# First loads in another order, a warm-up on TensorE, and the bias rows last, in a four-layer graph network kernel

## The chip, the cores and the metric

The kernel runs on one core of one Trainium2 chip. The metric is the device time of one execution in microseconds. The kernel before takes 1088.81 us (median of 3 runs, 1088.4 to 1089.32).

## The reference, cut to what matters

The reference puts 256 nodes with 768 features through four graph layers, each followed by `x = layernorm(x + layer(x))`. Only the very beginning of the first layer matters here, and four of its inputs:

```python
# 4352 edges: src, dst (0..255), edge_type_3 (0..2), edge_type_34 (0..33)
c = segment_sum(m.astype(x.dtype), dst)              # per relation: edges that end in a node
...
qg = einsum('blf,gf->blg', q, Wg[:, F:]) + bg        # q: query_embs, 8 x 64 rows of 768
hg = einsum('bnf,gf->bng', h3, Wg[:, :F])
attn = sigmoid(hg[:, :, None, :] + qg[:, None, :, :])
```

The kernel starts with two things that need nothing else: the query product `qg` (512 rows by 768, times 768 by 768, plus the bias `bg`) and the matrix of edge counts (destination by source, 256 x 256, for each of three relations).

## The kernel before, in words

Every engine has its own program, written out by hand, and semaphores tie them together. No planner sets the order: what stands earlier in an engine's list is done earlier. SyncE (SP) issues nearly all loads; all of them go through one hardware queue.

**SP.** It first issues four loads of 17 KB into `keys` (`src`, `dst`, `t3`, `t34`; L331), then `qT[0]` (the first 256 query rows, turned; 768 KB; L354; this buffer shares its memory with `MT[0]`, the name in the profile), then the first weight `W[0]` in three column thirds of 768 KB (L363), then `qT[1]` (L354) and the next weight `W[1]` (2304 KB, L365). After that it waits for buffers to come free.

**VectorE (DVE).** It waits for the four key loads, turns them into float32 (L1512 to L1516), and builds two one-hot tables of 34 chunks: `S1` by source (L1518) and `E[1]` by destination, relations 0 and 1 packed into one number (L1519). Each pair of chunks raises `chunk_ready`. Then it builds `E[0]` for relation 2 (34 instructions, L1507), and then it unpacks the sums that TensorE left in banks 6 and 7: for each bank it runs L1529 (from PSUM), L1530 (from SBUF to SBUF), L1531 (with one input from PSUM), and raises `half_read`. Two additions (L1533, L1534) finish the counts. After these come the low halves of the query rows (L1548, `query_lo`), the normalised counts (L1539 to L1541), a low half of x (L1562), another table of one-hots (L1507), tables for the last layer (L1567 to L1577), `query_lo` again, and the low halves L1555.

**TensorE (PE).** It waits for `bg_ready`, adds the bias into banks 0 to 5 by eight small products (L618), multiplies `qT[0]` by `W[0]` third by third (`natural3`, L581, 36 products that the trace shows as 72 records), raises `q_done`, adds up the counts of the chunks into banks 6 and 7 (L629, 68 matmuls), waits for `half_read`, and does the same for relation 2 in bank 6 (L637, 68 matmuls). Then come the sums of the counts (L643), the second half of the query product (L581) with one more sum in its middle (L569, which waits until the first two relations are normalised), and the first product of the layer (L668).

**ScalarE (ACT).** It rounds the bias (L1198), then waits for `q_done` and for `W[1]`, and splits off the high parts of the first two thirds of `W[1]` (L1193), then of x (L1205), and copies the query rows (L1207).

**GpSimd (POOL).** It makes constants: `iotab` (L395, raises `consts` to 1), masks and the identity (L397 to L417). It takes the low part of the bias (L421, raises `bg_ready`), waits for the last third of `W[0]` (`w_in[0]`), loads x (L424, L425), and then computes the low parts of the thirds of `W[1]`, as soon as ACT has made the high ones (`third_lo_first`, L430, whole inputs and output in SBUF, 128 x 1536).

`keep_busy(count, bank)` issues that many matmuls of 128 x 256 on the index table `iotab`; nobody reads what they leave.

Of the kernel before, what the change touches and what calls it, by code (L numbers as in the profile page):

```python
# [38 lines left out]
NODES, FEAT, EDGES = 256, 768, 4352  # L39
NT = NODES // P  # L40
KC = FEAT // P
EC = EDGES // P
# [36 lines left out]
def by_pool(n):  # L79

    return (n + 1) // 4
R3, R34 = 3, 34
HEADS1 = 4
SLOPE, MASKED = 0.2, 1e30
# [2 lines left out]
THIRD = FEAT // 3  # L87
# [10 lines left out]
def build(nc, A):  # L98
    with ExitStack() as ctx:
# [3 lines left out]
        def sem(name):  # L103
            return ctx.enter_context(nc.semaphore(name))


        PS = ctx.enter_context(nc.psum_tensor("PS", [P, 8, 512], F32))
        at_w = (nc.sbuf_base + 63) // 64 * 64
        W = [sb(f"W{i}", [P, KC, FEAT]) for i in range(2)]
# [4 lines left out]
        hN, hT = sb("hN", [P, NT, FEAT]), sb("hT", [P, KC, NODES])  # L114
# [5 lines left out]
        BG = nc.alloc_sbuf_tensor_at("BG", [33, FEAT], F32R, offset=at_h + 1024 * 20)  # L120
# [18 lines left out]
        keys = sb("keys", [P, 4, EC], I32)  # L139
# [110 lines left out]


        keys_in, x_in, bg_in, small_in, out_done = (sem(n) for n in ("keys_in", "x_in", "bg_in", "small_in", "out_done"))
        q_in = [sem("q_in0"), sem("q_in1")]
        first_in = [sem("first_in0"), sem("first_in1")]
        w_in = [sem("w_in0"), sem("w_in1")]
        rel_w_in = [[sem(f"rel_w_in{j}{q}") for q in range(2)] for j in range(2)]
        qd_in = [sem("qd_in0"), sem("qd_in1")]
# [69 lines left out]
        @block.sync  # L327
        def _(sp):

            for i, n in enumerate(("src", "dst", "t3", "t34")):  # L330
                sp.dma_start(keys[:, i, :], A[n].rearrange("(p c) -> p c", c=EC)).then_inc(keys_in, 16)  # L331
            def queries(g, u, h):

                for j in range(4):
                    sp.dma_start(QD[h][HQ * j:HQ * j + HQ, :], A["qU"][u, HQ * h:HQ * h + HQ]).then_inc(qd_in[h], 16)

            for m, w in enumerate(stream):
                if m in (6, 13):
                    g = m // 13
                    if g == 0:  # L340
                        sp.wait_ge(slot_found, EC)
                    else:
                        sp.wait_ge(wl_used, 3 * (R3 + 1))
                    for h in range(2):
                        queries(g, 0, h)
                if m in (9, 16):
                    g = m // 16
                    for u, h in product(range(1, UNITS), range(2)):
                        past = g * STEPS + (u - 1) * UB + (h + 1) * QUADS
                        sp.wait_ge(prod_done, by_dve(past))  # L350
                        sp.wait_ge(pool_prod, by_pool(past))
                        queries(g, u, h)
                if m < 2:
                    sp.dma_start(qT[m][:], turned(A["qT"])[:, :, m * NODES:(m + 1) * NODES]).then_inc(q_in[m], 16)  # L354
                elif m in (3, 4, 5, 6):
                    sp.wait_ge(wr_used, 3 * (m - 2))
                    sp.sem_inc(w_used, 1)
                else:
                    sp.wait_ge(w_used, m - 1)
                if m == 0:  # L360
                    for q in range(3):
                        cols = slice(q * THIRD, (q + 1) * THIRD)
                        sp.dma_start(W[0][:, :, cols], turned(w)[:, :, cols]).then_inc(w_in[0] if q == 2 else first_in[q], 16)  # L363
                else:
                    sp.dma_start(W[m % 2][:], turned(w)).then_inc(w_in[m % 2], 16)  # L365
            for n in range(2 * R34):
                r, q = divmod(n, 2)
                if n < 4:
                    if q == 0:
                        sp.wait_ge(w_used, FIRST34 - 1 + r)  # L370
                else:
                    sp.wait_ge(w_lo, n - 3)
                cols = slice(q * HALF, (q + 1) * HALF)
                sp.dma_start(W[(FIRST34 + r) % 2][:, :, cols], turned(A["L3_rel"][r])[:, :, cols]).then_inc(rel_w_in[r % 2][q], 16)
            m = FIRST34 + R34
            sp.wait_ge(w_lo, 2 * R34 - 2)
            sp.dma_start(W[m % 2][:], turned(A["L3_gcn"])).then_inc(w_in[m % 2], 16)

            for t in range(NT):
                sp.wait_ge(ln_done, 2 * 3 + t + 1)  # L380
                sp.dma_start(A["out"][t * P:(t + 1) * P, :], xN[:, t, :]).then_inc(out_done, 16)
            sp.wait_ge(out_done, 16 * NT)
# [110 lines left out]
        def _(pe):  # L493
# [3 lines left out]
            def keep_busy(count, bank):  # L497

                for _ in range(count):
                    pe.matmul(PS[:, bank, 0:NODES], iotab[:, 0:P], iotab[:], start=True, stop=True)  # L500
# [68 lines left out]
                    mm = pe.matmul(PS[:, bank, 0:NODES], ones[:], cnt[:, s, :], start=s == 0, stop=s == NT - 1)  # L569
                mm.then_inc(deg_spread, 1)  # L570

            def natural3(T, Wm, bank=0, first=False, last=False, tiles=range(NT), thirds=range(3), ready=None):

                for t in tiles:
                    for q in thirds:
                        at = 3 * t + q
                        out = PS[:, bank + at // 2, (at % 2) * THIRD:(at % 2 + 1) * THIRD]
                        for k in range(KC):
                            if ready and at == 0 and k % 2 == 0:
                                ready(k // 2)  # L580
                            mm = pe.matmul(out, T[:, k, t * P:(t + 1) * P], Wm[:, k, q * THIRD:(q + 1) * THIRD],  # L581
                                           start=first and k == 0 and at % 2 == 0,
                                           stop=last and k == KC - 1 and at % 2 == 1, skip_group_check=True)
                return mm

            def aggregate(n, x, nrm):
# [25 lines left out]
                return mm  # L612


            pe.wait_ge(bg_ready, 1)
            for u in range(2):
                for bank, at, f, n in ((0, 0, 0, 512), (1, 0, 512, 256), (1, 256, 0, 256), (2, 0, 256, 512)):
                    pe.matmul(PS[:, 3 * u + bank, at:at + n], ROWS2[:], BG[:, f:f + n], start=at == 0, stop=False,  # L618
                              skip_group_check=True)
            pe.wait_ge(q_in[0], 16)  # L620
            for q in range(3):
                pe.wait_ge(w_in[0] if q == 2 else first_in[q], 16)
                mm = natural3(qT[0], W[0], last=True, thirds=[q])
            mm.then_inc(q_done, 1)
            for c in range(EC):
                h, i = divmod(c, EHALF)
                pe.wait_ge(chunk_ready, c + 1)
# [14 lines left out]
            for s in range(NT):  # L642
                mm = pe.matmul(PS[:, 7, :], ones[:], CNT[:, 0:2, s, :], start=s == 0, stop=s == NT - 1)  # L643
            mm.then_inc(deg_spread, 2)
            pe.wait_ge(q_in[1], 16)
            natural3(qT[1], W[0], bank=3, last=True, tiles=[0])
            spread_counts(2, CNT[:, 2], bank=7)
            natural3(qT[1], W[0], bank=3, last=True, tiles=[1]).then_inc(w_used, 1)
            pe.wait_ge(qg_ready, 4)
# [50 lines left out]
            for g in range(2):  # L700
# [49 lines left out]
                weights(m0 + 4)  # L750
                if g == 0:
                    pe.wait_ge(slot_found, EC)
                natural3(hT, W[(m0 + 4) % 2], bank=3, first=True, last=True,
                         ready=lambda j: pe.wait_ge(relu_done, 3 * g + j + 1)).then_inc(w_used, 1)
                if g == 0:
                    sort_edges()
# [1333 lines left out]
```

## Time and profile before

| | |
|---|---|
| median of 3 runs | 1088.81 us |
| profiled execution | 1089.91 us |
| its span, first to last instruction | 1088.2 us |
| PE busy | 1039.5 us (96%) |
| DVE busy | 764.1 us (70%) |
| ACT busy | 573.4 us (53%) |
| POOL busy | 263.4 us (24%) |
| mean granted TensorE clock | 0.994 |

All rows come from one profiled execution. Times are counted from the first instruction. "Busy" counts an engine from the start to the modelled end of its instructions, so a busy PE may still be slow. The change is at the start, so the views of the first 85 us are the ones to read: which engine the chain of waits runs over, and what each engine waited for.

### The profile page before, as it was taken

To read this page: it belongs to the slowest core of one execution; us is meant where nothing else is said; L and a number is where in the kernel's file an instruction comes from. 1 tells how busy PE (TensorE), PEld (TensorE's weight loads), DVE (VectorE), ACT (ScalarE), POOL (GpSimd) and SP (SyncE) were. 2 spreads that over 40 slices of the span, in tenths; PEclk is the share of its full clock that TensorE was granted. 3 is DMA by queue.
4 is the path that set the end of the run, shared out by engine and by line. 5 is a ranking of instruction groups with operands and counts; after the bars stand their busy time and mean duration, and the time that the engine had idled before them with its cause. 6 is when DMAs were issued, how large, how long until landed. Compare 5 with 4: busy or idle time off the path is not lost.

```text
span 1088.2 us, 17713 instructions
## 1 busy us (share of the span) xinstructions
PE 1039.5 (96%) x7444; PEld 858.3 (79%) x7444; DVE 764.1 (70%) x1092; ACT 573.4 (53%) x606; POOL 263.4 (24%) x160
## 2 busy tenths in 40 slices
PE   6999999999999999999999989989999999999987
PEld 5889986454699984455879689956999999999974
DVE  8793855888654238887644584745989998989862
ACT  0432226888533248887324363324667676766630
POOL 3524705999300038996100000000000000000000
PEclk9999999999999999999999999999999999999999
DMA  8043247212043373220424302604978787877830
GB/s 296 12 135 129 88 149 230 59 59 59 2 174 123 119 220 130 60 59 20 160 88 175 117 1 87 246 11 138 304 256 283 256 284 256 270 261 263 276 118 29
DMA packets 82291, 163.18 MB, mean 150 GB/s; under 512 B 4044, under 2 KB 60136, under 8 KB 81918
## 3 DMA queue, kind: packets, MB, share of 16 engines
q1 hardware_dynamic: 80736, 151.86, 41.4%
q0 software_dynamic: 1472, 10.15, 3.4%
q8 instruction: 60, 0.98, 0.4%
q14 instruction: 23, 0.19, 0.1%
HBM read 158.35 MB, written 0.80 MB: 146 GB/s over the span
## 4 chain that ended last, share of the span: by engine, by line
PE 80%; DVE 13%; issue 4%; ACT 2%; POOL 1%; DVEq 0%; POOLq 0%; ACTq 0%
PE PS L1089 20%; PE PS L770 8%; PE PS L941 7%; PE PS L786 5%; PE PS L692 5%; PE PS L581 4%; PE PS L1072 4%; PE PS L511 4%; PE PS L668 4%; PE PS L524 3%; PE PS L593 3%; PE PS L1105 2%; PE PS L1006 2%; PE PS L828 2%; DVE PRD L1677 1%
## 5 line engine op out<-in xcount | busy, mean ns | idle before, releaser
L1926 DVE TENSOR_TENSOR Wlo<-W,Whi 128x2304 fp32r<-128x2304 f32 x68 | 172.1, 2551 | 19.0 <-ACT Whi L1425 19.0
L1425 ACT CAST Whi<-W 128x2304 fp32r<-128x2304 f32 x68 | 144.5, 2127 | 0.2 <-DMA W<-in_L_rel 0.2
L1089 PE MATMUL PS<-Whi,Mhi 128*128 128x384 f32 x408 | 138.0, 338 | 0.0
L1089 PE MATMUL PS<-Wlo,Mhi 128*128 128x384 f32 x408 | 136.5, 335 | 0.0
L1089 PE MATMUL PS<-Whi,Mlo 128*128 128x384 f32 x408 | 136.5, 334 | 0.0
L478 POOL TENSOR_TENSOR PRDP<-arena 128x1024 f32<-128x1024 f32 x48 | 114.8, 2391 | 30.1 <-issue 17.9
L770 PE MATMUL PS<-QH,SEL 128*128 128x512 f32 x384 | 115.7, 422 | 5.3 <-ACT xT L1262 1.4
L1283 ACT ACTIVATE arena<-PS 128x1024 f32<-128x1024 f32 x96 | 98.4, 1025 | 23.6 <-PE PS L770 23.5
L770 PEld LDWEIGHTS PS<-QH,SEL 128*128 128x128 f32 x384 | 64.8, 188 | 55.2 <-DVE PRD L1677 21.3
L1283 ACT ACTIVATE PS<-PS 128x1024 f32<-128x1024 f32 x96 | 97.9, 1019 | 2.6 <-PE PS L770 2.6
L1089 PEld LDWEIGHTS PS<-Whi,Mhi 128*128 128x128 f32 x408 | 76.8, 188 | 0.4 <-DVE Wlo L1926 0.2
L1089 PEld LDWEIGHTS PS<-Whi,Mlo 128*128 128x128 f32 x408 | 76.9, 188 | 0.0
L1089 PEld LDWEIGHTS PS<-Wlo,Mhi 128*128 128x128 f32 x408 | 76.6, 188 | 0.0
L1677 DVE TENSOR_TENSOR PRD<-PS,arena 128x1024 f32<-128x1024 f32 x48 | 58.5, 1220 | 19.7 <-ACT PS L1283 19.7
L1677 DVE TENSOR_TENSOR arena<-PS,arena 128x1024 f32<-128x1024 f32 x48 | 58.6, 1220 | 11.7 <-ACT PS L1283 11.7
L941 PE MATMUL PS<-WThi,Thi 128*128 128x256 f32 x216 | 61.5, 285 | 0.7 <-DVE Tlo L1804 0.7
L430 POOL TENSOR_TENSOR WR<-W,WH 128x1536 fp32r<-128x1536 f32 x12 | 48.6, 4058 | 52.3 <-ACT WH L1193 52.3
L941 PE MATMUL PS<-WThi,Tlo 128*128 128x256 f32 x216 | 61.1, 283 | 0.0
L941 PE MATMUL PS<-WTlo,Thi 128*128 128x256 f32 x216 | 61.1, 283 | 0.0
L1437 ACT CAST Mhi<-PS 128x512 fp32r<-128x512 f32 x51 | 30.0, 588 | 54.5 <-PE PS L1072 54.5
L1794 DVE TENSOR_TENSOR WTlo<-W,WThi 128x1536 fp32r<-128x1536 f32 x18 | 31.6, 1756 | 33.6 <-ACT WThi L1337 33.6
L1072 PE MATMUL PS<-BB,Xhi 128*128 128x256 f32 x204 | 52.0, 289 | 0.5 <-DVE Mlo L1955 0.5
(296 smaller groups left out, 2430.3 us busy)
## 6 DMA issues: line engine op xcount, KB each, us to landing
W<-in_L_rel SPq DMA_DIRECT2D x68, 1152.0 KB, 6.4
W<-in_W_rel SPq DMA_DIRECT2D x6, 2304.0 KB, 9.3
W<-in_W SPq DMA_DIRECT2D x6, 2304.0 KB, 9.4
arena<-in_qU SPq DMA_DIRECT2D x96, 128.0 KB, 2.6
W<-in_WqT SPq DMA_DIRECT2D x4, 2304.0 KB, 9.7
W<-in_W_root SPq DMA_DIRECT2D x2, 2304.0 KB, 13.5
W<-in_WgT SPq DMA_DIRECT2D x2, 2304.0 KB, 9.7
QH<-QH POOLq DMA_DIRECT2D x2, 1536.0 KB, 9.9
```

The costliest lines, as they stand in the source:

```text
L430: nc.gpsimd.tensor_tensor(part, third_turned(W[(1 + w // 3) % 2], w % 3), WH[(w + 1) % 3][:].bitcast(F32), ALU.subtract).then_inc(wr_ready, 1)
L478: nc.gpsimd.tensor_tensor(PRDP[k % 2], SIGP, QD[h], ALU.mult).then_inc(pool_prod, 1)
L692: mm = pe.matmul(PS[:, q, c * NODES:(c + 1) * NODES], WL[b][w % 2][:, k, c, :], TS[a][:, k, :], start=p == 0 and k == 0 and a == b == 0 an ...
L770: mm = pe.matmul(PS[:, at_banks(c) + b // 2, :], SEL[:, i, :], QH[h][:, u, b:b + 2, :].rearrange("p b f -> p (b f)"), start=True, stop=True)
L786: mm = pe.matmul(PS[32 * b:32 * b + 32, 6 + u % 2, 0:THIRD], RED[:, i % QUADS, :], made[:, b * THIRD:(b + 1) * THIRD], start=i == 0, stop= ...
L941: mm = pe.matmul(PS[:, bank + at // 2, (at % 2) * THIRD:(at % 2 + 1) * THIRD], TS[a][:, k, t * P:(t + 1) * P], WT[b][w % 2][:, k, :], star ...
L1072: mm = pe.matmul(PS[:, 6 + i % 2, kk * NODES:(kk + 1) * NODES], XS[part][:, t, k * P:(k + 1) * P], BB[:, t * NODES:(t + 1) * NODES], start ...
L1089: mm = pe.matmul(PS[:, 4 + s % 2, 0:HALF], MS[a][mb][:, k, j * P:(j + 1) * P], WS[b][w % 3][:, k, :], start=n == 0, stop=n == 17)
L1283: nc.scalar.activation(out, sums, ACT.Sigmoid).then_inc(attn_done, 1)
L1425: nc.scalar.copy(WS[0][w % 3][:], W[(FIRST34 + r) % 2][:, :, q * HALF:(q + 1) * HALF]).then_inc(w_hi, 1)
L1677: V.tensor_tensor(PRD[k % 4], sig, QD[h], ALU.mult).then_inc(prod_done, 1)
L1926: V.tensor_tensor(WS[1][w % 3][:], W[(FIRST34 + r) % 2][:, :, q * HALF:(q + 1) * HALF], WS[0][w % 3][:].bitcast(F32), ALU.subtract).then_i ...
```

## The change

In SP's program the first loads are `qT[0]` and the first third of `W[0]` for the first two of six feature blocks (256 KB each), then the four key loads, then the other four blocks of both, then the second and the last third of `W[0]`. In TensorE's program 16 filler matmuls into bank 7 come first. They wait for `iotab` alone. The query product follows, its first third in two pieces, and the eight bias products stand at its end, where `bg_ready` is now waited for. Bank starts are given by the new argument `opens`. In the code below, `natural3` has no `first` any more.

```diff
+FIRST_KS = (range(2), range(2, KC))
...
-        q_in = [sem("q_in0"), sem("q_in1")]
-        first_in = [sem("first_in0"), sem("first_in1")]
+        q_in, third_in = sem("q_in"), sem("third_in")
+        first_in = [sem(f"first_in{j}") for j in range(2)]
...
-            for i, n in enumerate(("src", "dst", "t3", "t34")):
-                sp.dma_start(keys[:, i, :], A[n].rearrange("(p c) -> p c", c=EC)).then_inc(keys_in, 16)
...
-                if m < 2:
-                    sp.dma_start(qT[m][:], turned(A["qT"])[:, :, m * NODES:(m + 1) * NODES]).then_inc(q_in[m], 16)
+                if m == 1:
+                    sp.dma_start(qT[1][:], turned(A["qT"])[:, :, NODES:2 * NODES]).then_inc(q_in, 16)
+                elif m == 0:
+                    for j, ks in enumerate(FIRST_KS):
+                        ks = slice(ks[0], ks[-1] + 1)
+                        sp.dma_start(qT[0][:, ks, :], turned(A["qT"])[:, ks, 0:NODES]).then_inc(first_in[j], 16)
+                        sp.dma_start(W[0][:, ks, 0:THIRD], turned(w)[:, ks, 0:THIRD]).then_inc(first_in[j], 16)
+                        if j == 0:
+                            for i, n in enumerate(("src", "dst", "t3", "t34")):
+                                sp.dma_start(keys[:, i, :], A[n].rearrange("(p c) -> p c", c=EC)).then_inc(keys_in, 16)
...
                 if m == 0:
-                    for q in range(3):
+                    for q in range(1, 3):
                         cols = slice(q * THIRD, (q + 1) * THIRD)
-                        sp.dma_start(W[0][:, :, cols], turned(w)[:, :, cols]).then_inc(w_in[0] if q == 2 else first_in[q], 16)
+                        sp.dma_start(W[0][:, :, cols], turned(w)[:, :, cols]).then_inc(w_in[0] if q == 2 else third_in, 16)
...
-            pe.wait_ge(bg_ready, 1)
-            for u in range(2):
-                for bank, at, f, n in ((0, 0, 0, 512), (1, 0, 512, 256), (1, 256, 0, 256), (2, 0, 256, 512)):
-                    pe.matmul(PS[:, 3 * u + bank, at:at + n], ROWS2[:], BG[:, f:f + n], start=at == 0, stop=False,
-                              skip_group_check=True)
-            pe.wait_ge(q_in[0], 16)
-            for q in range(3):
-                pe.wait_ge(w_in[0] if q == 2 else first_in[q], 16)
-                mm = natural3(qT[0], W[0], last=True, thirds=[q])
-            mm.then_inc(q_done, 1)
+            pe.wait_ge(consts, 1)
+            keep_busy(16, 7)
+            for j, ks in enumerate(FIRST_KS):
+                pe.wait_ge(first_in[j], 32)
+                natural3(qT[0], W[0], opens=(0, 3), thirds=[0], ks=ks)
+            pe.wait_ge(third_in, 16)
+            natural3(qT[0], W[0], opens=(4,), thirds=[1])
+            pe.wait_ge(w_in[0], 16)
+            natural3(qT[0], W[0], thirds=[2])
             pe.wait_ge(bg_ready, 1)
+            bias_rows(0, False)
+            bias_rows(3, True).then_inc(q_done, 1)
```

## Rows read from the trace of the kernel before

**Rows 1.** The page, part 1: busy time, share of the span, instructions.
```profile
PE 1039.5 (96%) x7444; PEld 858.3 (79%) x7444; DVE 764.1 (70%) x1092; ACT 573.4 (53%) x606; POOL 263.4 (24%) x160
```
**Rows 2.** The chain of waits, 0 to 84 us: start, duration, what.
```profile
9.89 2.92 PE PS L618 x8
12.82 17.70 PE PS L581 x72
30.51 7.44 PE PS L629 x68
...
81.55 1.99 PE PS L593 x8
```
**Rows 3.** Timeline, 5 to 42 us, VectorE: start, duration, line, operation, idle before.
```profile
4.78 0.23 DVE L1512 CAST keyf<-keys 128x136 f32<-128x136 int32 x1 [3.84 <-DMA keys<-in_t]
8.11 1.82 DVE L1518 TENSOR_SCALAR S<-iotab,keyf 128x256 bf16<-128x256 bf16 x1
23.72 6.75 DVE L1507 TENSOR_SCALAR E<-iotab,ekey 128x256 bf16<-128x256 bf16 x34
34.26 0.69 DVE L1529 TENSOR_SCALAR NRM<-PS 128x512 f32<-128x512 f32 x1 [3.79 <-PE PS L629]
34.99 0.85 DVE L1530 TENSOR_SCALAR CNT<-NRM 128x512 f32<-128x512 f32 x1
...
37.97 0.69 DVE L1529 TENSOR_SCALAR NRM<-PS 128x512 f32<-128x512 f32 x1 [1.41 <-PE PS L629]
38.70 0.73 DVE L1530 TENSOR_SCALAR NRM<-NRM 128x512 f32<-128x512 f32 x1
41.62 7.11 DVE L1548 TENSOR_TENSOR QH<-PS,QH 32x1536 fp32r<-32x1536 f32 x4
```
**Rows 4.** DMA, 0 to 60 us: issues, KB each, median us to landing.
```profile
W<-in_WgT SPq DMA_DIRECT2D x3, 768.0 KB, 9.3
W<-in_W_root SPq DMA_DIRECT2D x1, 2304.0 KB, 18.3
```
**Rows 5.** Timeline, the first 12 us, SP: start of issue, duration.
```profile
0.81 0.38 SPq L331 DMA_DIRECT2D keys<-in_src  x1
2.65 0.43 SPq L354 DMA_DIRECT2D MT<-in_qT  x1
```
**Rows 6.** Line 354, both loads of qT: the time to landing.
```profile
DMA to landing us min/median/max: 5.6/8.2/10.7
```
**Rows 7.** Timeline, 30 to 40 us, ScalarE.
```profile
30.55 2.85 ACT L1193 CAST WH<-W 128x1536 fp32r<-128x1536 f32 x2 [25.18 <-PE PS L581]
```
**Rows 8.** Timeline, GpSimd, 5 to 11 and 30 to 40 us.
```profile
7.94 1.90 POOL L421 TENSOR_TENSOR BG<-biasN,BG 1x768 fp32r<-1x768 f32 x1
32.11 7.03 POOL L430 TENSOR_TENSOR WR<-W,WH 128x1536 fp32r<-128x1536 f32 x2 [14.64 <-ACT WH L1193]
```
**Rows 9.** Line 430, whole span: duration ns min/median/max, first and last start.
```profile
L430 POOL TENSOR_TENSOR WR<-W,WH x12: 3437/3486/10267, 32.1 to 128.4; 128x1536 fp32r<-128x1536 f32 x12
```
**Rows 10.** Timeline, 112 to 132 us: VectorE, then GpSimd.
```profile
114.53 4.68 DVE L1617 TENSOR_TENSOR PROW<-iota,t34f 128x4352 bf16<-128x4352 f32 x1
119.13 2.55 DVE L1619 TENSOR_TENSOR PCOL<-iota,t34f 128x2312 bf16<-128x2312 f32 x1
...
114.72 17.16 POOL L430 TENSOR_TENSOR WR<-W,WH 128x1536 fp32r<-128x1536 f32 x3
```
**Rows 11.** Windows: us, busy PE, PEld, DVE, ACT, POOL, granted clock, DMA.
```profile
13.00:14.00 1.00, 1.00 (x3) 0.82 (x4) 1.00 (x6) 0.00 (x0) 0.00 (x0) 1.00 1.10 347
18.00:19.00 1.00, 1.00 (x6) 0.87 (x6) 1.00 (x6) 0.00 (x0) 0.00 (x0) 1.00 1.02 390
...
307.00:308.00 1.00, 1.00 (x6) 1.00 (x6) 1.00 (x1) 0.00 (x0) 0.00 (x0) 0.50 1.01 409
```
**Rows 12.** Timeline, TensorE, around 306 us and around 55 us.
```profile
306.22 0.39 PE L692 MATMUL PS<-Thi,WLhi 128*128 128x256 f32 x1 [1.85 <-DVE Tlo L1705]
...
54.69 1.10 PE L569 MATMUL PS<-CNT,ones 128*128 128x256 f32 x4
```

More of the change, by code:

```diff
@@ L570, in spread_counts, with natural3 @@
                 mm.then_inc(deg_spread, 1)
-            def natural3(T, Wm, bank=0, first=False, last=False, tiles=range(NT), thirds=range(3), ready=None):
+            def natural3(T, Wm, bank=0, opens=(), last=False, tiles=range(NT), thirds=range(3), ks=range(KC), ready=None):
                 for t in tiles:
@@ L577, in natural3 @@
                         out = PS[:, bank + at // 2, (at % 2) * THIRD:(at % 2 + 1) * THIRD]
-                        for k in range(KC):
+                        for k in ks:
                             if ready and at == 0 and k % 2 == 0:
@@ L581, in natural3, with bias_rows @@
                             mm = pe.matmul(out, T[:, k, t * P:(t + 1) * P], Wm[:, k, q * THIRD:(q + 1) * THIRD],
-                                           start=first and k == 0 and at % 2 == 0,
+                                           start=k == 0 and at in opens,
                                            stop=last and k == KC - 1 and at % 2 == 1, skip_group_check=True)
+                return mm
+            def bias_rows(bank, opens):
+                for b, at, f, n in ((0, 0, 0, 512), (1, 0, 512, 256), (1, 256, 0, 256), (2, 0, 256, 512)):
+                    mm = pe.matmul(PS[:, bank + b, at:at + n], ROWS2[:], BG[:, f:f + n], start=opens and at == 0,
+                                   stop=not opens and (b, at) != (1, 0), skip_group_check=True)
                 return mm
@@ L644, in _ @@
             mm.then_inc(deg_spread, 2)
-            pe.wait_ge(q_in[1], 16)
-            natural3(qT[1], W[0], bank=3, last=True, tiles=[0])
+            pe.wait_ge(q_in, 16)
+            natural3(qT[1], W[0], bank=3, tiles=[0])
             spread_counts(2, CNT[:, 2], bank=7)
@@ L752, in _ @@
                     pe.wait_ge(slot_found, EC)
-                natural3(hT, W[(m0 + 4) % 2], bank=3, first=True, last=True,
+                natural3(hT, W[(m0 + 4) % 2], bank=3, opens=(0, 2, 4), last=True,
                          ready=lambda j: pe.wait_ge(relu_done, 3 * g + j + 1)).then_inc(w_used, 1)
```

## The prediction
> **What bounds the kernel now.** I read the page first: TensorE is busy for 96% of the span [rows 1], so it looks like the bound everywhere. The change touches only the first 40 us, and there the chain of waits says more. It runs over TensorE up to 37.95 us (bias products from 9.89, query product from 12.82 to 30.51, count sums 7.44 us) and then passes to VectorE; it comes back to TensorE only at 81.55 us, at L593 [rows 2]. Between these two points the chain is one row after another of VectorE, without a gap. So TensorE's start is worth only what it brings forward on VectorE at 38 us. What is saved there goes through to L593, and after 81.55 us TensorE hardly waits.
>
> The VectorE timeline shows where the slack is: it waits 3.84 us for the keys, and 3.79 us for bank 6 before L1529 [rows 3]. Before the second L1529, for bank 7, it waits 1.41 us more [rows 3]. Together 5.2 us is all that an earlier TensorE can give.
>
> **TensorE's side.** The filler starts once `iotab` stands, near 1.8 us. A warm L629 takes 7.44 / 68 = 0.109 us from one to the next [rows 2]; at half the clock 0.22, so 16 take 3.5 us, to 5.3 us. The rate before shows the cold start: 3 records in a microsecond at 13 us, 6 at 18 us [rows 11], so the product runs at 1.2 GHz until about 17 us although TensorE began at 9.89. Warm, a record takes about 0.216 us from one to the next, so a product (two records) takes 0.43, and the 72 records 15.5 us instead of 17.7 [rows 2].
>
> The data come as follows. `qT[0]`, issued at 2.65, landed 5.6 us later, at 8.25 [rows 5, 6], which is the shortest of the two times. The middle third of `W[0]` took 9.3 us from its issue [rows 4] and landed near 13.0; the thirds came 2.3 us apart (10.7, 13.0, 15.3), the time of 768 KB in a full queue. Now the stream starts with the first big load at 0.81 instead of 2.65 (1.8 us earlier), and the keys are put into it (about 0.6 us): everything after them lands about 1.2 us earlier, the last third near 14.1. The first piece lands near 5.5, and its 4 products are done before the second piece lands near 9.5. From there the work binds: 32 products of 0.43 us, to 23.3, then the bias products, 2.92 us before at the low clock [rows 2], half of that warm: `q_done` near 24.7 instead of 30.5. The chunk sums end near 32.1 instead of 37.95, and bank 6 is ready near 28.4.
>
> **VectorE's side, the keys.** The four key loads were issued from 0.81 on, 0.46 us apart, and had landed for L1512 at 4.78 [rows 3, 5]. Now two issues of that length stand ahead of them (0.9 us) and 512 KB in the same queue. The bounds are 0.9 us later (issue alone) and 3.5 us (landing at 8.25, like `qT[0]` with more bytes ahead). By the rate of the first loads, about 270 GB/s, 512 KB are 1.9 us from about 2.6 us on; with 0.6 for the keys and the time to landing that gives 5.9 instead of 4.7: 1.2 us later. VectorE gets about 0.2 back, because fewer of its first instructions meet GpSimd's masks. I take the tables to end 1.0 us later: L1507's table at T = 31.5 instead of 30.47 [rows 3].
>
> If nothing else happened, VectorE would go on at T without waiting: 2 x 1.95 us for the two banks and 1.3 us for the additions, and L1548 would start at T + 5.3 = 36.8 instead of 41.62: a gain of 4.8 us.
>
> **What is late next: GpSimd's two instructions of L430.** I think that this gain is lost. L430 stands after ACT's L1193, and that waited for `q_done` until 30.55 [rows 7]. `W[1]` had landed at 9.16 + 18.3 = 27.5 [rows 4]. With `q_done` at 24.7 the load decides: it lands near 26.5, ACT's first copy takes 1.47, and L430 is issued near 28 us, in the middle of VectorE's table. In the rows before, these two engines exclude each other for some operations: L1518 took 1.82 us, against 0.28 for its neighbours, beside L421 (7.94 to 9.84) [rows 3, 8]; L1530 took 0.85 and 0.73 us, and each ended 0.29 us after the end of one of the two L430 (about 35.56 and 39.14) [rows 3, 8]. L1530 (SBUF to SBUF) is hit; L1529 and L1531, which read PSUM, are not. The one-hots of L1507 are the same form as L1518.
>
> Who goes first? At 114.72 an L430 was issued beside L1617, and L1619 was started while L1617 ran; GpSimd took 10.27 us in place of 3.49 [rows 9, 10], so it got in only at 121.5, when both were over. VectorE's unbroken run kept it out. L1507 is such a run. So the first L430 gets in at T and holds to T + 3.45. VectorE: L1529 to T + 0.75; L1530 waits and ends at T + 3.75; L1531 to T + 4.45, `half_read`. The second L430 gets in after L1530 and ends near T + 7.2; the second L1530 ends near T + 7.45. From there to L1548 it is 41.62 - (38.70 + 0.73) = 2.2 us as before [rows 3]: T + 9.6 = 41.1 instead of 41.62. **The gain on VectorE is 0.5 us.** ACT's query copies are done by then.
>
> The Trainium skill (SBUF — State Buffer, Who interferes with whom) has this as an exclusive lock on a port pair that VectorE and GpSimd share, held for a whole instruction: copies, casts and tensor_scalar in the two-port modes take it, and "Issue order, not op shape, decides who blocks". The blocked rows agree. By issue order alone L430 would get in at 28 us, between two one-hots; that is the second rival, and the row at 114.72 speaks against it.
>
> **TensorE again.** It is idle from 32.1 to T + 4.5 = 36.0, 3.9 us. At 306.22 it had waited 1.85 us and the clock then stood at 0.50 for about 3.4 us [rows 11, 12], which costs 1.7. The sums L637 then end at 36.0 + 7.4 + 1.7 = 45.1, as before (they began near 37.7, when L629 ended). L569 started at 54.69 [rows 12], when VectorE had just normalised relation 1; TensorE gets there no earlier than before, so VectorE's third L1539 loses 0.1 us of its gain. Without the drop of the clock all 0.5 us stay; with twice the price 1.3 us are lost instead. I take 0.4 us.
>
> The sum: the profiled execution of 1089.91 (span 1088.2) becomes 1089.5; it lay 1.1 us above the median. The median 1088.81 becomes **1088.4 us**. About 0.2% (2.2 us) is what a measurement of this kernel can tell from no change.
>
> **Rivals.**
> *No blocking worth the name.* The two L430 slip past both L1530. For it: the blocking is inferred from five rows, and between two instructions of VectorE there may be room that no row here shows. Against it: the two L430 are 6.9 us of GpSimd, and from their issue at 28 us to the last addition of VectorE there are only 9 us. VectorE gains 4.8 us; TensorE gains less, 33.8 instead of 37.7 at L637, and if its clock drops in the 1.7 us gap, 2.2 us. VectorE's third L1539 waits for L569 and follows: a gain of 2.5 to 4.2 us, 1084.6 to 1086.3, say 1085.3.
>
> *GpSimd gets in first* (the other side). The first L430 takes the pair at 28 us and stalls the table for 3.45 us: T becomes 34.9. The second waits for the end of the run and hits L1530: `half_read` at T + 4.5 = 39.4 instead of 36.6, L637 starts 1.75 us later than before, cold after 7 us of idling (1.7 more). L569 and the third L1539 are then 3.1 us late, and that reaches L593 over VectorE [rows 2]: 1088.8 + 3.1 = 1091.9. It decides as soon as one L430 starts inside the L1507 run. If both do, 1093.
>
> *The first piece lands late.* Then the filler only fills and the product starts near 9.5 as before; TensorE has 3.9 us to spare before `half_read`, so the time is that of the forecast. It is inside it.
>
> **How the numbers follow.** The forecast 0.55 (own range 1086.7 to 1090.3: keys 0.9 to 3.5 us later shift T by as much, and the clock costs 0 to 3.4 us), no blocking 0.30, GpSimd first 0.15. The range of 8 in 10 reaches half into both: 1084.8 to 1091.0. Faster by over 0.2%: 0.30. Within: 0.55. Slower: 0.15.
>
> **What would show it.** L1512 near 6.0 us. The end of the query product (ACT's L1193 no longer waits for it) near 24.7. L430 issued near 28 us with a duration near 7 us instead of 3.45 (if GpSimd gets in first: a duration of 3.45, and one L1507 of 3.5 us). The first L1530 near 3 us long. L637 at 36. L1548 near 41.1. Wrong if L1548 starts before 39 or after 43, or if the shift at 41.6 us is not the one at L593.

## The result, and the profile after

The changed kernel takes 1093.38 us (median of 6 runs, 1091.58 to 1094.83), the kernel before 1088.90 beside it (6 runs, 1088.02 to 1089.35): ratio 1.0041, 95% interval [1.0030, 1.0052]. It is 4.5 us **slower**. The forecast was 1088.4, no change; the result lies above its range (1084.8 to 1091.0) and on the figure of the second rival with both low parts inside the table (1093). The change is small, 0.4%, but the interval keeps clear of 1.

The profiled execution is the fastest of the six (1091.58, span 1089.8). Read it for the first 90 us. The delay found there lasts nearly to the end: SyncE issues its last weight load at 1045.71 us, 3.9 us after the kernel before (1041.81). In the last 45 us this execution won 2.2 us back. The change touches nothing there, and executions of one kernel differ by 1.3 to 6 us here; why these two differ at that place is open.

The page's part 1, after. Beside [rows 1] VectorE is busy for 6.1 us more, with the same 1092 instructions: some of them take longer.
```profile
PE 1041.8 (96%) x7460; PEld 858.2 (79%) x7460; DVE 770.2 (71%) x1092; ACT 573.4 (53%) x606; POOL 262.9 (24%) x160
```
The chain of waits, 25 to 90 us, after (start, duration, what).
```profile
25.60 13.27 DVE E L1523 x34
...
40.86 9.40 PE PS L653 x68
50.26 1.73 PE PS L659 x4
...
54.27 2.11 DVE NRM L1557
...
86.22 1.99 PE PS L607 x8
```
This part of the chain starts on VectorE (before it stands the keys' load, up to 7.11 us, and VectorE's work on the keys), with the table of 34 one-hots (L1507 before, L1523 here) at almost twice its 6.75 us. At the end stands the product that began at 81.55 [rows 2]; here it begins at 86.22, **4.67 us later**, about what the medians differ by.

VectorE's timeline, 3 to 56 us, after (start, duration, line, operation, idle before). The lines answer to L1512, L1516, L1507, L1529 to L1531, L1548 and L1541 before.
```profile
7.21 0.23 DVE L1528 CAST keyf<-keys 128x136 f32<-128x136 int32 x1 [6.28 <-DMA keys<-in_t]
8.04 1.66 DVE L1532 TENSOR_SCALAR ekey<-keyf 128x34 f32<-128x34 f32 x1
...
38.79 0.68 DVE L1545 TENSOR_SCALAR NRM<-PS 128x512 f32<-128x512 f32 x1
39.51 0.43 DVE L1546 TENSOR_SCALAR CNT<-NRM 128x512 f32<-128x512 f32 x1
...
41.53 0.43 DVE L1546 TENSOR_SCALAR NRM<-NRM 128x512 f32<-128x512 f32 x1
...
44.15 7.11 DVE L1564 TENSOR_TENSOR QH<-PS,QH 32x1536 fp32r<-32x1536 f32 x4
...
54.27 2.11 DVE L1557 TENSOR_TENSOR NRM<-CNT,RC 128x512 f32<-128x512 f32 x1
```
Both waits for TensorE are gone (3.79 and 1.41 us in [rows 3]), and both SBUF copies L1546 take 0.43 us, not 0.85 and 0.73. The step that the prediction was built on did not happen there. It happened earlier. First line L1523's own view, then the timeline of VectorE and GpSimd in two slices of a few tenths of a us:
```profile
L1523 DVE TENSOR_SCALAR E<-iotab,ekey x34: 273/274/3548, 25.6 to 38.6; 128x256 bf16<-128x256 bf16 x34
```
```profile
28.94 3.55 DVE L1523 TENSOR_SCALAR E<-iotab,ekey 128x256 bf16<-128x256 bf16 x1
28.96 3.44 POOL L437 TENSOR_TENSOR WR<-W,WH 128x1536 fp32r<-128x1536 f32 x1 [11.69 <-ACT WH L1209]
...
32.37 3.48 POOL L437 TENSOR_TENSOR WR<-W,WH 128x1536 fp32r<-128x1536 f32 x1
32.41 3.52 DVE L1523 TENSOR_SCALAR E<-iotab,ekey 128x256 bf16<-128x256 bf16 x1
```
The shortest, median and longest one-hot: 273, 274 and 3548 ns. Two of 34 took 3.5 us, and each ends within 0.1 us of the end of a low part. GpSimd got in at once, with 3.44 and 3.48 us. Between the two low parts VectorE got exactly one one-hot through.

TensorE, the first 51 us, after.
```profile
1.77 3.60 PE L507 MATMUL PS<-iotab 128*128 128x256 bf16 x16 [1.77 <-POOL iotab L402]
5.16 2.84 PE L588 MATMUL PS<-W,MT 128*128 128x256 f32 x8
10.00 15.77 PE L588 MATMUL PS<-W,MT 128*128 128x256 f32 x64 [2.00 <-DMA W<-in_WgT]
25.70 1.67 PE L596 MATMUL PS<-BG,ROWS 33*128 33x512 f32 x8
...
40.86 9.40 PE L653 MATMUL PS<-E,S 128*128 128x256 bf16 x68 [5.96 <-DVEq L1548]
```
The product and the bias rows end at 27.4, not at 30.5. TensorE then idles 5.96 us for the late table, and its 68 sums take 9.40 us. Windows over that wait (us, then busy PE, PEld, DVE, ACT, POOL, granted clock, DMA):
```profile
35.00:40.00 5.00, 0.00 (x0) 0.00 (x0) 4.93 (x19) 2.30 (x2) 0.85 (x1) 0.78 0.00 0
40.00:45.00 5.00, 4.14 (x22) 2.96 (x23) 4.61 (x7) 0.00 (x0) 0.00 (x0) 0.54 0.00 0
```
The clock falls to its lower level in the idle time: by single microseconds it is 0.90 from 37 to 38 us and 0.50 from 38 us on. It rises again between 44 and 45 us.

GpSimd's third low part, before and after:
```profile
47.49 3.44 POOL L430 TENSOR_TENSOR WR<-W,WH 128x1536 fp32r<-128x1536 f32 x1 [1.29 <-ACT WH L1193]
```
```profile
52.39 3.44 POOL L437 TENSOR_TENSOR WR<-W,WH 128x1536 fp32r<-128x1536 f32 x1 [1.30 <-ACT WH L1209]
```

**The account.** Up to L1564 (L1548 before): the table starts 1.88 us later (25.60 against 23.72), the collision adds 6.5 (13.27 against 6.75), the waits give back 3.79 and 1.41, and the two copies 0.42 and 0.30: +2.5, as measured (44.15 against 41.62). Then VectorE waits 0.77 us for TensorE's slow sums, and L1557 takes 2.11 us instead of 0.69, blocked by the *third* low part (52.39 to 55.83): +1.4. Together +4.7.

The last two terms both come from TensorE. In the program the third low part stands behind the sums of relation 2, and in both traces it starts 2.29 us after TensorE has begun the group behind these sums (45.20 to 47.49 before, 50.10 to 52.39 here). The block ends 0.55 us after the low part's end. So the end of L1557 can also be counted over TensorE: its sums start 3.09 us later than before (40.86 against 37.77), because the table is late, and take 1.81 us longer (9.40 against 7.59), because the clock is low. Before, L1541 ended 0.21 us later than such a block would have ended (51.69 against 51.48): 3.09 + 1.81 - 0.21 = 4.7. By this count the fall of the clock is 1.8 us of the 4.7; a3 below bears it out.

### The profile page after: what moved, and what is told of

Read it like the earlier page. It is cut to its first block, busy times and chain, and to the rows that moved or that the text cites. A ratio compares the mean times of both kernels' runs of the same rounds, so it can differ in the third digit from the quotient of the medians.

```text
span 1089.8 us, 17746 instructions
## 1 busy us (share of the span) xinstructions
PE 1041.8 (96%) x7460; PEld 858.2 (79%) x7460; DVE 770.2 (71%) x1092; ACT 573.4 (53%) x606; POOL 262.9 (24%) x160
## 3 DMA queue, kind: packets, MB, share of 16 engines
q0 software_dynamic: 1472, 10.15, 3.4%
## 4 chain that ended last, share of the span: by engine, by line
PE 77%; DVE 15%; issue 4%; ACT 2%; POOL 0%; DMA 0%; SPq 0%; DVEq 0%; ACTq 0%
PE PS L1105 20%; PE PS L786 8%; PE PS L957 7%; PE PS L802 5%; PE PS L1088 4%; PE PS L708 4%; PE PS L518 4%; PE PS L684 4%; PE PS L531 3%; PE PS L588 3%; PE PS L607 3%; PE PS L1121 2%; PE PS L1022 2%; DVE E L1523 2%; PE PS L844 2%
```

## The experiments

All but b1 and b2 start from the changed kernel. The last column but one is the start of VectorE's first Tlo instruction (L1555 before), the end of the stretch in which the chain runs over VectorE, against 80.80 in the kernel before. If the cause lies before it, the two last columns should go together, and they do, within 1.4 us, over a range of 10 us. (The shift of Tlo is that of one profiled execution, the other that of the medians; the 1.4 is e1's, whose profiled execution, 1084.74, was nearly its fastest.) "Before" was 1089.33 beside a1 to a4, 1089.19 beside c1 to d2, 1088.99 beside b1, b2, e1 and e2.

| kernel | median us | ratio [95%] | shift of Tlo us | shift of the median us |
|---|---|---|---|---|
| changed kernel | 1093.38 | 1.0041 [1.0030, 1.0052] | +4.68 | +4.5 |
| a1 hold behind the table | 1088.96 | 1.0000 [0.9991, 1.0008] | -0.58 | -0.4 |
| a2 hold behind the additions | 1086.24 | 0.9973 [0.9963, 0.9984] | -3.28 | -3.1 |
| a3 keys first | 1091.05 | 1.0016 [1.0005, 1.0028] | +0.98 | +1.7 |
| a4 two-scalar one-hots | 1095.08 | 1.0053 [1.0041, 1.0065] | +6.19 | +5.8 |
| b1 before + new loads alone | 1089.50 | 1.0007 [0.9998, 1.0016] | +0.38 | +0.5 |
| b2 before + hold | 1089.99 | 1.0011 [1.0003, 1.0020] | +1.23 | +1.0 |
| c1 keys first + hold | 1087.64 | 0.9987 [0.9978, 0.9996] | -2.31 | -1.6 |
| c2 keys from ScalarE's queue + hold | 1087.97 | 0.9993 [0.9984, 1.0002] | -2.23 | -1.2 |
| d1 34 tensor_tensor (one execution) | 1091.77 | | +4.92 | |
| d2 2 tensor_tensor (one execution) | 1094.17 | | +5.75 | |
| e1 hold, third low part earlier | 1086.57 | 0.9976 [0.9967, 0.9985] | -3.79 | -2.4 |
| e2 a tile in TensorE's gap | 1095.65 | 1.0055 [1.0038, 1.0072] | (chain on TensorE) | +6.7 |

### Is it the collision? a1 and a2

GpSimd's first two low parts are held by one wait, behind the table or behind the additions.
```diff
+            pool.wait_ge(e_ready, R3)       # a1;  a2: pool.wait_ge(cnt_copied, 2)
             third_lo_first(0)
             third_lo_first(1)
```
Expected of a1:

> The changed kernel, with GpSimd's first low part (third_lo_first, L437) held until the one-hot table of relation 2 is finished. Theory L (the table lost 6.5 us to GpSimd's two instructions): no instruction of the table lasts over 0.3 us, the table ends at 32.3 us instead of 38.8; now the two low parts meet both L1546, as I forecast for the changed kernel, so the query rows (L1564) start near 41.8 instead of 44.15. Time 1089 to 1090, some 3.5 to 4.5 us under the changed kernel. Theory K (the late keys and the low clock are the loss, the long one-hots are only where VectorE would have waited anyway): under 1.5 us better than the changed kernel, 1092 or more.

Expected of a2:

> The changed kernel, with the same instruction of GpSimd held until VectorE has finished the counts (cnt_copied at 2), so that neither the table nor L1546 meets it. Theory L: the table ends at 32.3, L1564 starts near 37.6, TensorE's second sums start near 34.9 without a long idle time. The third low part then may meet L1557 (up to 1.2 us). Time 1085 to 1087, faster than the kernel before. Theory K: the keys are still 1.9 us late, so at best 1090.

VectorE's timeline in a1, from the table on:
```profile
24.74 6.75 DVE L1524 TENSOR_SCALAR E<-iotab,ekey 128x256 bf16<-128x256 bf16 x34
31.41 0.68 DVE L1546 TENSOR_SCALAR NRM<-PS 128x512 f32<-128x512 f32 x1
32.13 3.16 DVE L1547 TENSOR_SCALAR CNT<-NRM 128x512 f32<-128x512 f32 x1
...
36.88 1.98 DVE L1547 TENSOR_SCALAR NRM<-NRM 128x512 f32<-128x512 f32 x1
```
and in a2, up to the third low part's block:
```profile
34.37 0.43 DVE L1547 TENSOR_SCALAR NRM<-NRM 128x512 f32<-128x512 f32 x1
...
36.99 7.11 DVE L1565 TENSOR_TENSOR QH<-PS,QH 32x1536 fp32r<-32x1536 f32 x4
...
46.38 2.04 DVE L1558 TENSOR_TENSOR NRM<-CNT,RC 128x512 f32<-128x512 f32 x1
```
a1 forces the course that the prediction took for granted (low parts at the table's end), and gets it: the table in 6.75 us, the first copy 3.16 us long, the low halves at 41.05 (predicted 41.1), time 1088.96 (predicted 1088.4). One term of the prediction doesn't show: TensorE waits 3.25 us before the sums of relation 2, but they take 7.58 us, at the full clock, and not 1.7 more. a2 takes the whole collision away: low halves at 36.99, where the prediction, without any blocking, had put 36.8; 1086.24 us. One wait on GpSimd, all else being equal, is worth 4.4 us in the one place and 7.1 in the other: **the collision is the cause**, shown. (That includes what hangs on it: with the table on time, TensorE's sums start earlier and run at the full clock in both kernels. Of the shift of Tlo, 0.9 and 0.6 us are keys that landed earlier in these two profiled executions.)

### Which half of the change? a3, b1 and b2

a3 puts the four key loads back to the front of the queue. b1 has the new order of loads with the old TensorE program (bias rows first, no filler). b2 is the kernel before with the wait of a2.
```diff
# a3
+            for i, n in enumerate(("src", "dst", "t3", "t34")):
+                sp.dma_start(keys[:, i, :], ...).then_inc(keys_in, 16)
             def queries(g, u, h):
...
-                        if j == 0:
-                            for i, n in enumerate(("src", "dst", "t3", "t34")):
-                                sp.dma_start(keys[:, i, :], ...).then_inc(keys_in, 16)
# b1
-            pe.wait_ge(consts, 1)
-            keep_busy(16, 7)
+            pe.wait_ge(bg_ready, 1)
+            bias_rows(0, True)
+            bias_rows(3, True)
```


> The changed kernel with the four key loads in front again; the pieces, the warm-up and the bias rows stay as changed. Theory L: the table starts 1.9 us earlier but still meets both low parts and ends near 37.0; L1564 near 42.3. Time 1091 to 1092, 1.5 to 2 us under the changed kernel and still slower than the kernel before. Theory K: most of the loss is gone, 1089 or less.

> The kernel before with the new order of loads alone; TensorE's program is the old one (bias rows first, no filler). Theory (the loss comes from GpSimd's two low parts falling into the table of 34 one-hots, and that needs the earlier TensorE): the keys land near 7.1 us instead of 4.7, the table ends 1.9 us later, at 32.4, but the query product ends near 30.5 as before, so the two low parts start near 32, behind the table. VectorE's wait of 3.79 us before its first unpacking swallows the 1.9 us: the low halves of the query rows start at 41.6 plus or minus 0.3, time 1088.9 within 1 us. Rival (the later keys are a loss by themselves): 1090.8 or more.

> The kernel before, with GpSimd's first two low parts held until the counts are unpacked (the wait of the kernel with held additions, 1086.24). Theory: the two small blocked unpackings (0.85 and 0.73 us instead of 0.43) lose 0.7 us; TensorE is still late, so nothing else is won: 1088.2, unless the third low part then blocks a copy near 52 us, which takes it back (1089). Rival (holding GpSimd is worth something by itself, whatever TensorE does): 1086.5 or less.

The table in a3, then the first unpacking after the table in b1, both from VectorE's timeline:
```profile
23.73 13.26 DVE L1522 TENSOR_SCALAR E<-iotab,ekey 128x256 bf16<-128x256 bf16 x34
```
```profile
24.85 6.75 DVE L1521 TENSOR_SCALAR E<-iotab,ekey 128x256 bf16<-128x256 bf16 x34
34.66 0.69 DVE L1543 TENSOR_SCALAR NRM<-PS 128x512 f32<-128x512 f32 x1 [3.05 <-PE PS L643]
```
In a3 the keys are early and the collision is all there (13.26): still slower than before, as expected. The late keys are worth 2.3 us of the changed kernel's 4.5 (1093.38 against 1091.05). Between the two profiled executions it is 3.7 us, and only 1.9 of them are the table's later start. The rest is the clock. TensorE's sums of relation 2 in a3:
```profile
38.98 7.58 PE L652 MATMUL PS<-E,S 128*128 128x256 bf16 x68 [3.85 <-DVEq L1547]
```
After 3.85 us without work they run at the full clock (granted 1.00), after 5.96 us in the changed kernel they start at 0.50 and take 1.8 us more. 1.88 + 1.82 is the 3.70 by which Tlo differs.

In b1 the late keys cost nothing that can be measured (1.0007, and the interval holds 1): the table is whole (6.75), and of its 1.13 us of delay 0.74 goes into the wait for TensorE, 3.05 us instead of 3.79; the other 0.4 is TensorE's own, whose sums ended later. So the new order of loads alone is harmless. The earlier TensorE alone is not: a3 loses 1.7 us, because the low parts start inside the table. Together they lose more, since the earlier TensorE also takes away the slack that hid the late keys.

b2 missed both expectations, 1088.2 and 1089. The wait did free the two copies (0.43 us each), but TensorE is late there, nothing was won, and the third low part slid to 48.92 and hit a normalisation in the chain (L1541 in the kernel before):
```profile
50.90 2.03 DVE L1542 TENSOR_TENSOR NRM<-CNT,RC 128x512 f32<-128x512 f32 x1
```
2.03 against 0.69 us: +1.3, and Tlo is 1.23 us late. Holding GpSimd is no gain by itself; it moves the collision.

### Why did the table not keep GpSimd out? a4, d1 and d2

The prediction took one row for a rule: two tensor_tensor of VectorE in a row kept GpSimd waiting [rows 10]. These three write the same 34 one-hots with other instructions: a4 as tensor_scalar with a second scalar operand, d1 as 34 tensor_tensor, d2 as 2 tensor_tensor of 17 chunks each.
```diff
-            onehot(E[0], ekey[:, 0, :]).then_inc(e_ready, R3)
+            for c in range(EC):                      # d1 (d2: 17 chunks at once, a4: V.tensor_scalar
+                ins = V.tensor_tensor(E[0][:, c, :], iotab[:],     #  with ones[:, 0:1], ALU.mult)
+                                      ekey[:, 0, c:c + 1].to_broadcast([P, NODES]), ALU.is_equal)
+            ins.then_inc(e_ready, R3)
```


> The changed kernel, with the 34 one-hots of relation 2 written in the form of L1535 (two scalars from SBUF, the second one is 1.0): 0.26 us from one to the next instead of 0.20. GpSimd is not held. Theory L (it is a port that this form does not use): none of them is blocked, the table takes 34 x 0.26 = 8.8 us in place of 13.3 and ends near 34.3, GpSimd's two instructions keep 3.44 us each. L1564 near 39.7, time 1088 to 1089.5. If GpSimd stopped VectorE by something else (memory traffic, a semaphore), the long instructions would stay and the time would be 1093 or more.

> The changed kernel with the 34 one-hots of relation 2 as 34 tensor_tensor instructions with two inputs from SBUF (0.27 us each), GpSimd not held. It tells why L430 had to wait behind L1617 and L1619 in the kernel before, but gets in between one-hots. Theory 'kind': a run of tensor_tensor keeps GpSimd out: no long instruction, the table ends near 34.5, GpSimd's first low part takes about 9 us. Theory 'gap': GpSimd gets in at the end of whatever instruction runs: one instruction of 3.5 us near 29 and another one behind it, the table ends near 41, GpSimd keeps 3.44 us.

> The same with two tensor_tensor instructions of 17 chunks each (4.6 us), as L1617 and L1619 are. Theory 'kind': GpSimd waits for both, table ends near 34.3. Theory 'gap': GpSimd is issued near 29, inside the first one (25 to 29.8) or just at its end, gets in when it ends, and the second one lasts 4.6 + 3.4 us or more; table ends near 38 to 41.

The one-hot's own line and then GpSimd's, in a4, d1 and d2 (duration ns min/median/max):
```profile
L1542 DVE TENSOR_SCALAR E<-iotab,ekey,ones x34: 327/334/3545, 24.6 to 39.5; 128x256 bf16<-128x256 bf16 x34
```
```profile
L1541 DVE TENSOR_TENSOR E<-iotab,ekey x34: 414/417/424, 25.0 to 36.1; 128x256 bf16<-128x256 bf16 x34
...
L437 POOL TENSOR_TENSOR WR<-W,WH x3: 3434/3594/10145, 29.7 to 52.6; 128x1536 fp32r<-128x1536 f32 x3
```
```profile
L1541 DVE TENSOR_TENSOR E<-iotab,ekey x2: 4694/6312/7930, 25.2 to 29.9; 128x4352 bf16<-128x4352 bf16 x2
...
L437 POOL TENSOR_TENSOR WR<-W,WH x3: 3437/5178/7855, 28.1 to 53.5; 128x1536 fp32r<-128x1536 f32 x3
```
In a4 two of the one-hots take 3.5 us again (3.54 and 3.52): the two-scalar form is hit just like the other, and my expectation that it would pass was wrong. In d1 none does (424 ns at most), and it is GpSimd that waits: its first low part, issued at 29.67, takes 10.15 us and ends 3.3 us after the table. That is [rows 10] again, with instructions as small as the one-hots. So a difference in the size of the instructions or in the room between two of them (the records overlap by 0.08 us in both forms) doesn't explain it; the kind of operation went with it: **the runs of tensor_scalar let GpSimd in within one instruction, this run of tensor_tensor did not.** But in d2 a run of tensor_tensor did let it in: the first one took 4.69 us, GpSimd (issued at 28.06) got in at its end, and the second took 7.93. What decides between d1 and [rows 10] on one side and d2 on the other stays open; d1 and d2 are one execution each.

d1 also shows that keeping GpSimd out would not have saved this change: the instructions are slower (11.49 us for 34), the low part then hits the copy behind the table (2.93 us), and Tlo is as late as in the changed kernel.

### What do TensorE's late and slow sums cost? e2

The first tile of the second query half moves in front of the 68 sums, into the 6 us of idle time.
```diff
+            pe.wait_ge(q_in, 16)
+            natural3(qT[1], W[0], bank=3, tiles=[0])
             pe.wait_ge(e_ready, R3)
             pe.wait_ge(half_read, 1)
...
-            pe.wait_ge(q_in, 16)
-            natural3(qT[1], W[0], bank=3, tiles=[0])
```


> The changed kernel with the first tile of the second query half moved in front of the sums of relation 2, into TensorE's idle time of 6 us (34.9 to 40.9). Theory (after the collision the chain runs over VectorE; TensorE's cold clock costs little): TensorE stays warm, the sums take 7.6 us instead of 9.4 and start near 42.6; VectorE's course up to the low halves of the query rows at 44.1 is unchanged; the counts of relation 2 come at the same time, the block of 2.11 us at the copy near 54 stays or moves: 1093.0, range 1091.5 to 1093.8. Rival (TensorE's late and slow sums carry a good part of the loss): 1090.5 or less, since 7.7 us of TensorE's work is done in idle time.

TensorE's timeline in e2:
```profile
34.38 7.94 PE L588 MATMUL PS<-W,MT 128*128 128x256 f32 x36
42.15 7.59 PE L655 MATMUL PS<-E,S 128*128 128x256 bf16 x68
...
58.82 2.04 PE L576 MATMUL PS<-CNT,ones 128*128 128x256 f32 x4 [7.36 <-DVE NRM L1557]
60.66 9.72 PE L588 MATMUL PS<-W,MT 128*128 128x256 f32 x36
```
The gap before the sums is filled and they run at the full clock (7.59 us), as both theories said. But the tile ends later than the gap: the sums start 1.3 us later than in the changed kernel (42.15 against 40.86), so they are over only 0.5 us earlier (the next group starts at 49.57, against 50.10), and the third low part blocks L1557 again (2.09 us). And the tile had been the cover of another wait, that of L576 for VectorE's normalised counts. Without it TensorE idles 7.36 us there, its clock falls at that place instead, and the next product takes 9.72 us instead of 7.93. The median lies 2.3 us above that of the changed kernel, but the two intervals overlap ([1.0038, 1.0072] and [1.0030, 1.0052]), so that e2 is slower is likely, not shown. The expectation (1091.5 to 1093.8) missed because it looked at the sums alone. What e2 shows is that this tile can't use the idle time for a gain. It doesn't price the late and slow sums, since it hardly moved their end. Their price is in the two traces of a3 and the changed kernel: 1.8 us for the clock alone.

### Can the gain be kept? c1, c2 and e1

All three have the wait of a2. c1 has the keys first as well; c2 issues the keys from ScalarE's queue and moves the relation table's load behind the third low part; e1 does only the latter.
```diff
# c2
+                act.dma_start(keys[:, i, :], ...).then_inc(keys_in, 16)
# c2, e1
+            third_lo_first(2)
             pool.wait_ge(cnt_summed, R3)
             pool.dma_start(RELT[:], ...).then_inc(rel_in, 16)
-            third_lo_first(2)
```


> The changed kernel with the keys in front and GpSimd's low parts held until the counts are finished (the two former edits together). The table of relation 2 ends at 30.5, but TensorE's chunk sums end only near 35 (the pieces land 1.5 us later, the clock rose at 13 us with the keys in front), so VectorE waits for bank 7: L1563 near 38, against 37.0 with the keys late and GpSimd held. If the port theory is right the two edits don't add up: 1086 to 1087.5. If each loss stood by itself: 1083.9, the 2.4 us of the keys on top of the 1086.2.

> A version that tries to have both: SP starts with the pieces, ScalarE issues the four key loads on its own queue at its very start, GpSimd's low parts are held until the counts are finished, and the load of RELT is moved behind the third low part. Expected: keys at 5.5 to 6 us, TensorE as in the changed kernel (q_done near 25), table ends near 31, L1564 near 36.3, the third low part blocks L1557 for 0.9 us instead of 1.35. Time 1084.5 to 1086. If ScalarE's table load or the shared DMA engines delay the keys to 7 us as before, 1086.

> The changed kernel with held low parts (1086.24), and in addition GpSimd's issue of the relation table's load moved behind the third low part, so that this part starts near 44 us only if the wait before it was the load's, and else directly behind the second at 43.9. Theory: the third low part still meets VectorE near 46.4 us, so little is won: 1086.0, range 1085.3 to 1086.8. Rival: the block of 2.04 us at 46.4 goes away whole and the time falls by 1.4 us, to 1084.8.

The first instruction on the keys in c2; then in c1 VectorE's first unpacking; then the normalisation that the third low part blocks, in e1:
```profile
8.52 1.52 DVE L1528 CAST keyf<-keys 128x136 f32<-128x136 int32 x1 [7.59 <-DMA keys<-in_t]
```
```profile
30.91 0.69 DVE L1545 TENSOR_SCALAR NRM<-PS 128x512 f32<-128x512 f32 x1 [0.68 <-PE PS L645]
...
34.62 0.69 DVE L1545 TENSOR_SCALAR NRM<-PS 128x512 f32<-128x512 f32 x1 [1.83 <-PE PS L645]
```
```profile
46.45 1.47 DVE L1558 TENSOR_TENSOR NRM<-CNT,RC 128x512 f32<-128x512 f32 x1
```
With the keys first TensorE's data are late and VectorE waits 0.68 and 1.83 us for it: c1 is not better than a2, and its 1087.64 lies just above the expected 1086 to 1087.5 and far from the 1083.9 of losses that add up. So once GpSimd is out of the way, keys behind the first piece cost nothing against keys in front. In c2 the keys on a queue of their own came later still (8.5 us), although ScalarE issued them from 0.81 us on, a microsecond earlier than SyncE in the changed kernel (1.80); why is open. c2's expectation (1084.5 to 1086) was wrong. e1 came as expected (1085.3 to 1086.8): it shortens the block from 2.04 to 1.47 us and Tlo by 0.5, but its median is no lower than a2's; the two can't be told apart. **a2 and e1 beat both kernels**, by 0.27% and 0.24% against before.

## Why the prediction was wrong

- **Where to look**: right in the main. Chain of waits over TensorE to 38 us, then VectorE to 81.5, and what is late at Tlo goes through to the end; the table above shows it over 10 kernels. But the shift at 41.6 us is not the one at L593, +2.5 against +4.7: VectorE is tied to TensorE's sums once more at 54 us, by way of the third low part. The text had named both this and an L1548 after 43 (44.15) as signs of being wrong.
- **TensorE's side**: right in kind, late in size. Filler to 5.3 (measured 5.4), first piece at 5.2 (5.5 predicted). The second piece came at 10.0 (9.5), and the product ended at 25.8 instead of 23.3. The warm-up did not last in this execution: after 2.00 us without work the granted clock was 0.50 from 11 to 13 us, and the 64 records took 15.77 us. In a1, a2, a4, d2 and e1 they took 14.08, after waits of 1.15 to 2.46 us, and ended between 23.4 and 23.9 as forecast; what decides is open. (In [rows 11] the granted clock reads 1.00 at 13 us as well; the slow start of the kernel before is read from the records, 3 in a microsecond instead of 6.) It made little difference: `W[1]`, issued at 8.81, took 18.4 us to landing (27.2), `q_done` came at 27.4, and ScalarE started at 27.41, so the low parts came at 28.96 (predicted 28). Both of VectorE's waits went, as predicted.
- **The keys**: predicted 1.2 us later, and the table 1.0. Measured in this execution 2.43 and 1.88; in the other eight kernels with this order of loads and the same queue the table started between 24.61 and 25.34, 0.9 to 1.6 us later. The term was somewhat small, and it varies from run to run.
- **The step that failed** is this one: "VectorE's unbroken run kept it out. L1507 is such a run. So the first L430 gets in at T". It was drawn from two tensor_tensor [rows 10] and applied to 34 tensor_scalar. GpSimd got in at the first chance, twice, and the table took 13.27 us instead of 6.75. a1 shows VectorE's part of the sum to be sound: with the low parts held to T it ran the predicted course to 0.1 us.
- **The rival** had it: "one L1507 of 3.5 us", T at 34.9 for one, 1093 for both. The size is partly luck, since the text gives no working for the 1093. Its path was right in kind: the sums late (3.09 us, with both low parts in the table), then cold (1.81). But it let them reach VectorE by L569; they reached it by the third low part, which it didn't have.
- **The Trainium skill** (SBUF — State Buffer, Who interferes with whom) was set aside in favour of one row. Its rule, "Issue order, not op shape, decides who blocks", gives the right time for the one-hots and for a4. It doesn't give d1, where the shape was a one-hot's, the low part was issued in the middle of the run, and GpSimd waited 6.7 us; there the measurement decides.
- **The clock**: 1.7 us was the price of a fall (it was 1.8 here, 9.40 instead of 7.6 us), but the forecast took a fall for granted after 3.9 us of waiting. In a1 and a3, after 3.25 and 3.85 us, the clock stayed at 1.00 and the sums took 7.58. It fell after the longer wait of the changed kernel (5.96), and there the 1.8 us went through whole.
- **Not seen at all**: the third low part. It was in the trace before (47.49 to 50.93, beside a reciprocal that doesn't mind, and its end 0.07 us before L1541 at 51.00). Where GpSimd falls behind VectorE by more than that, it is a block of up to 1.4 us. It was one in the changed kernel and in all the others but a1 and b1.

The chance of 0.15 for this rival was too low. The only evidence against it was one row of another kind of instruction, and there were rows for it: L1518, the one-hot's own form, had been blocked by L421 [rows 3, 8], in the midst of an unbroken run.

## What to carry to other kernels

When a change brings one engine forward, list what it *triggers* on the others, and look where that lands: here a TensorE that was 3 us earlier sent two GpSimd instructions of 3.4 us into a run of VectorE instructions that cost 0.2 us each, and the late table then cost TensorE its clock (1.8 us); one wait on GpSimd turned a loss of 4.5 us into a gain of 3. Before you take a row as a rule of who goes first, find one of the same operation: the row of the blocked one-hot was there. And a late input costs nothing only as long as the wait behind it stands; two edits of one change can each take away the other's cover.

## What was not expected of the hardware

- VectorE and GpSimd alternate one for one between tensor_scalar one-hots (0.27 us) and low parts (3.44 us). The short ones pay: 3.5 us each, 6.5 us for two.
- 34 tensor_tensor of 0.42 us kept GpSimd out for 6.7 us, two of 4.6 us did not (one execution each); open.
- The same 68 products took 7.58 us after TensorE had waited 3.85 us, and 9.40 us, at a granted clock of 0.50 at first, after 5.96 us.
- Four loads of 17 KB on a queue of their own (ScalarE's, issued from 0.81 us) were used at 8.5 us, in one trace; behind 512 KB in SyncE's queue they were used at 5.9 to 7.2, and in front of it at 4.8.
